# Two-layer transformer/Mamba kernel on eight cores: a second projection pass dropped, reciprocals moved into the score loop, and the Mamba input matmuls run ahead

## What is computed

```python
# layer 0, attention (16 heads of 64), after a layer norm of x
Z = query @ Wz + bz
Z = (Z - mu) * rsqrt(var + 1e-5) * ln_g + ln_b
Q, R, Hv = Z @ Wq + bq, Z @ Wr + br, Z @ Wh + bh        # per head
Qc = concat([Q*cos(Q@Wphi+bphi), Q*sin(Q@Wphi+bphi)])   # Rc alike from R
scores = Qc @ Rc^T
out = (scores / max(sqrt(sum(scores**2)), 1e-12)) @ Hv  # then @ Wo + bo
# layer 0 ffn: shared SwiGLU branch + 8 routed experts
# layer 1, two Mambas (m1 forward, m2 on the reversed sequence)
x, z = split(h @ Win)
x = silu(causal_conv4(x) + bconv)
dbc = x @ Wx;  dt = softplus(dbc[:, :32] @ Wdt + bdt)
h_t = exp(dt*A) * h_(t-1) + dt*B*x;   y = sum_n(h_t * C)   # 16 states
out = ((y + Dp*x) * silu(z)) @ Wout
# layer 1 ffn: int8-quantized product
```

## Time and profile before

| | us |
|---|---|
| median of 2 timed runs | 9415.58 |
| the two runs | 9391.38 and 9439.77 |
| profiled execution, its own time | 9415.49 |
| its span, first to last instruction, slowest core (core 3) | 9414.0 |
| spans of the 8 cores | 9384.4 to 9414.0 |
| busy PE / DVE / ACT / POOL | 4334.1 / 4807.9 / 3167.4 / 172.1 |
| mean granted clock of PE over all cores | 0.624 to 0.629 |

### The profile page before, as it was taken

One profiled execution on the slowest core, in us unless ns is written; L12 is line 12 of the kernel. 1 busy time (PEld: TensorE's weight loads), 2 busy tenths in 40 slices (PEclk: granted clock), 3 DMA queues, 4 the chain that ended last, 5 costly groups with the idle time before them and its releaser, 6 DMA issues.

```text
span 9414.0 us, 57603 instructions; the slowest of 8 cores (9384.4 to 9414.0 us)
## 1 busy us (share of the span) xinstructions
PE 4334.1 (46%) x11136; PEld 1254.8 (13%) x11136; DVE 4807.9 (51%) x8137; ACT 3167.4 (34%) x4433; POOL 172.1 (2%) x221
## 2 busy tenths in 40 slices
PE   3644564456447499994323232323233232323334
PEld 1211111111112142110000000000000000000112
DVE  2434443444444321225476766757575767767345
ACT  3333333333332221003342534434343534344321
POOL 0000000000000000000000000000000000000000
PEclk8766776676768796665555555555555555555556
DMA  1042682100000242110000000000000000000000
GB/s 45 5 38 23 70 84 25 18 0 4 4 0 10 58 128 74 54 45 0 11 7 16 4 17 3 16 7 13 12 9 14 5 18 3 15 6 13 26 11 36
DMA packets 203008, 222.94 MB, mean 24 GB/s; under 512 B 131441, under 2 KB 140049, under 8 KB 200561
## 3 DMA queue, kind: packets, MB, share of 16 engines
q0 software_dynamic: 141104, 76.50, 7.8%
q1 hardware_dynamic: 61570, 142.76, 4.6%
HBM read 278.07 MB, written 65.03 MB: 36 GB/s over the span
## 4 chain that ended last, share of the span: by engine, by line
DVE 39%; PE 31%; issue 14%; ACT 12%; DMA 2%; DVEq 1%; POOL 0%; ACTq 0%; SPq 0%; POOLq 0%
DVE HBF L1731 14%; PE P2U L200 10%; PE PSU L200 6%; DVE DBXP L1727 5%; PE P3U L200 3%; PE PSU L855 3%; PE PSU L866 3%; DVE SCBW L885 2%; DVE XCC L1456 2%; DVEq L35 1%; PE P3U L1783 1%; DVE CARRY L1736 1%; ACT L1655 1%; ACT SCBW L895 1%; PE P3U L1703 1%
## 5 line engine op out<-in xcount | busy, mean ns | idle before, releaser
L1703 PE MATMUL P3U<-DBXP,EYEB 128*128 128x512 bf16 x1024 | 580.1, 566 | 1967.2 <-DVE DBXP L1738 1967.0
L1731 DVE TENSOR_TENSOR_SCAN HBF<-DAP,CARRY,DBXP 128x512 bf16<-128x512 bf16 x1024 | 1314.4, 1284 | 109.3 <-DVE DBXP L1727 3.7
L885 DVE CAST SCBW<-PSU 128x512 bf16<-128x512 f32 x512 | 353.6, 691 | 532.1 <-PE PSU L855 526.8
L1727 DVE TENSOR_TENSOR DBXP<-U_CH,BREP 128x512 bf16<-128x512 bf16 x1024 | 428.8, 419 | 311.4 <-ACT DAP L1655 189.9
L855 PE MATMUL PSU<-QCB,RCB 128*128 128x512 bf16 x1024 | 434.3, 435 | 292.8 <-DVE REP L831 292.8
L866 PE MATMUL PSU<-SCBW,HV 128*64 128x512 bf16 x960 | 415.0, 432 | 196.6 <-DVE SCBW L885 165.0
L895 ACT CAST SCBW<-PSU 128x512 bf16<-128x512 f32 x512 | 300.2, 586 | 526.5 <-PE PSU L855 525.8
L200 PE MATMUL P2U<-YLN,W1E 128*128 128x512 bf16 x512 | 462.1, 1078 | 11.3 <-DMA W1E<-wfsc 11.3
L1667 ACT ACTIVATE DAP<-DT_CH,ACOL 128x512 bf16<-128x512 bf16 x512 | 358.9, 719 | 304.7 <-DVE HBF L1731 299.9
L1703 PEld LDWEIGHTS P3U<-DBXP,EYEB 128*128 128x128 bf16 x1024 | 107.5, 105 | 2448.1 <-issue 2447.9
L1738 DVE TENSOR_TENSOR DBXP<-HBF,CREP 128x512 bf16<-128x512 bf16 x1024 | 424.4, 414 | 1.9 <-issue 1.9
(11 more groups left out here) (324 smaller groups left out, 7176.6 us busy)
## 6 DMA issues: line engine op xcount, KB each, us to landing
wfsc<-L_ffn_w POOLq DMA_DIRECT2D x16, 2048.0 KB, 89.2
SW1H<-wfsc SPq DMA_DIRECT2D x64, 256.0 KB, 2.7
SW3H<-wfsc SPq DMA_DIRECT2D x64, 256.0 KB, 3.0
SW2C<-wfsc SPq DMA_DIRECT2D x32, 512.0 KB, 4.3
W1E<-wfsc SPq DMA_DIRECT2D x8, 2048.0 KB, 12.1
W2E<-wfsc SPq DMA_DIRECT2D x8, 2048.0 KB, 7.7
WINS<-wmsc SPq DMA_DIRECT2D x64, 256.0 KB, 2.6
WINZ<-wmsc SPq DMA_DIRECT2D x64, 256.0 KB, 2.6
```

The source lines that it names most:

```text
L885: b.sV.inc(v.tensor_copy(SCBW[kt % 2][:], PSU[kt % 2][:, :]))
L1703: b.sT.inc(t.matmul(ybank[:, :], EYEB[:], DBXP[ni % 2][:], start=(ni == 0), stop=(ni == 7)))
L1727: b.sV.inc(v.tensor_mul(DBXP[ni % 2][:], U_CH[:, dt * QC:(dt + 1) * QC], BREP[:, ni * QC:(ni + 1) * QC]))
L1731: b.sV.inc(v.tensor_tensor_scan(HBF[ni % 2][:], DAP[ni % 4][:], DBXP[ni % 2][:], CARRY[:, dt * 16 + n: dt * 16 + n + 1], ALU.mult, ALU.add))
```

## The change

It has three parts.

1. **Z stage.** The bf16 copy of Z goes into its place in `ZLN` rather than into `STB`. The statistics matmuls read it there. `_zb_t`, the second pass of 256 matmuls, is gone, and `_zb_v` multiplies the bf16 copy from SBUF by `REP`.
2. **Heads.** Square root, maximum and reciprocal of `RNREP` leave the head's start. Each query chunk does its own 512 columns behind its score casts and ahead of `_av_ev`, in blocks of their own. The mark in `pair_free` for ACT is taken behind the square root.
3. **Mamba.** PE issues the `Win` groups of all eight tiles first, over three `WINS` buffers and three banks (`PSU[0]`, `PSU[1]`, `PSU[3]`), and the eight products with `WXB` behind them (`_s1_t2`). There is one `XCC` and one `ZT` in place of two each, so a convolution waits for the SiLU before it.

```diff
@@ _za_t, _za_v, _zb_v
-                    b.sT.inc(t.matmul(PSU[0][0:1, :], ONECOL[:], STB[2 * (j % 2) + 1][:],
+                    qj, ej = divmod(j, KT)
+                    b.sT.inc(t.matmul(PSU[0][0:1, :], ONECOL[:],
+                                      ZLN[:, ej * T + qj * QC: ej * T + (qj + 1) * QC],
                                       start=(et == 0), stop=(et == KT - 1)))
...
-                    b.sV.inc(v.tensor_copy(STB[2 * (j % 2) + 1][:], ZCH[j % 2][:]))
+                    b.sV.inc(v.tensor_copy(ZLNt(et)[:, q * QC:(q + 1) * QC], ZCH[j % 2][:]))
...
-            b.t(_zb_t)
...
-                    b.sV.inc(v.scalar_tensor_tensor(ZCH[j % 2][:], PSU[2 + j % 2][:, :],
-                                                    BIAS[:, et:et + 1],
-                                                    REP[:, q * QC:(q + 1) * QC],
-                                                    ALU.add, ALU.mult))
+                    b.sV.inc(v.tensor_mul(ZCH[j % 2][:],
+                                          ZLNt(et)[:, q * QC:(q + 1) * QC],
+                                          REP[:, q * QC:(q + 1) * QC]))
@@ heads
-                    b.s(_rne_s)
-                    b.v(_rne_v)
...
                         prev_sc = (b.sV.n, b.sS.n)
+                        def _rnq_s(s, qc=qc):
+                            b.sS.wait(s)
+                            b.sS.inc(s.activation(RNREP[:, qc * QC:(qc + 1) * QC],
+                                                  RNREP[:, qc * QC:(qc + 1) * QC], AF.Sqrt))
+                        b.s(_rnq_s)
+                        rnq_m = b.sS.n
+                        def _rnq_v(v, qc=qc, rnq_m=rnq_m):
+                            b.sS.wait(v, rnq_m)
+                            b.sV.inc(v.tensor_scalar(RNREP[:, qc * QC:(qc + 1) * QC],
+                                                     RNREP[:, qc * QC:(qc + 1) * QC],
+                                                     C_TINY, None, ALU.max))
+                            b.sV.wait(v)
+                            b.sV.inc(v.reciprocal(RNREP[:, qc * QC:(qc + 1) * QC],
+                                                  RNREP[:, qc * QC:(qc + 1) * QC]))
+                        b.v(_rnq_v)
                         if hh == 1 and qc == NQ - 1:
                             pair_free[hp].append((b.sS, b.sS.n))
 
                         def _av_ev(v, qc=qc, hh=hh, hp=hp):
                             b.sT.wait(v)
                             b.sS.wait(v)
+                            b.sV.wait(v)
@@ Mamba stage 1
-                            elif dt >= 2:
-                                b.sT.wait(g, tb6 + 2 * (dt - 2) + 1)
+                            elif dt >= 3:
+                                b.sT.wait(g, tb6 + (dt - 3) + 1)
...
-                            b.sT.inc(mm_group(t, PSU[dt % 2][:, :],
-                                              [(WINS[dt % 2][:, kt * 128:(kt + 1) * 128],
+                            b.sT.inc(mm_group(t, XZB[dt % 3][:, :],
+                                              [(WINS[dt % 3][:, kt * 128:(kt + 1) * 128],
                                                 mv_h(kt, c0, QC)) for kt in range(KT)]))
                             st_tm[dt] = b.sT.n
-                            b.sS.wait(t, st_sm.get(dt, 0))
+
+                    def _s1_t2(t, st_sm=st_sm):
+                        for dt in range(KT):
+                            b.sS.wait(t, st_sm[dt])
                             b.sT.inc(t.matmul(PSU[2][0:64, :],
                                               WXB[:, dt * 64:(dt + 1) * 64],
...
-                            if dt >= 2:
-                                b.sS.wait(v, sb6 + dt - 1)
+                            if dt >= 1:
+                                b.sS.wait(v, sb6 + dt)
...
-                                    if dt >= 2:
-                                        b.sV.wait(s, gate3_m[dt - 2])
+                                    if dt >= 1:
+                                        b.sV.wait(s, gate3_m[dt - 1])
```

More of the change, by code:

```diff
@@ L521, in _za_v @@
                 for j in range(NJ):
+                    q, et = divmod(j, KT)
                     b.sS.wait(v, s_zevac_cnt(j))
-                    b.sV.inc(v.tensor_copy(STB[2 * (j % 2) + 1][:], ZCH[j % 2][:]))
+                    b.sV.inc(v.tensor_copy(ZLNt(et)[:, q * QC:(q + 1) * QC], ZCH[j % 2][:]))
             b.v(_za_v)
             ln_statmath_and_reps(PSU[2], denom=D)
-            z2tb, z2sb, z2vb = b.sT.n, b.sS.n, b.sV.n
-            presnap = b.snap()
-            zb_tm = {}
+            z2sb, z2vb = b.sS.n, b.sV.n
             zb_vm = {j: z2vb + 2 * (j + 1) for j in range(NJ)}
             zb_sm = {j: z2sb + j + 1 for j in range(NJ)}
[L534 to L543, removed]
-            b.t(_zb_t)
             def _zb_v(v):
@@ L814, in build_program @@
                     mm_evac(NQ, rn_mm, rn_ev, [PSU[0], PSU[1]], "s")
[L815 to L821, removed]
-                    b.s(_rne_s)
-                    def _rne_v(v, sb_rn=sb_rn):
-                        for qc in range(NQ):
-                            b.sS.wait(v, sb_rn + qc + 1)
-                            b.sV.inc(v.tensor_scalar(RNREP[:, qc * QC:(qc + 1) * QC],
-                                                     RNREP[:, qc * QC:(qc + 1) * QC],
-                                                     C_TINY, None, ALU.max))
-                            b.sV.wait(v)
-                            b.sV.inc(v.reciprocal(RNREP[:, qc * QC:(qc + 1) * QC],
-                                                  RNREP[:, qc * QC:(qc + 1) * QC]))
-                    b.v(_rne_v)
                     prev_sc = None
@@ L1360, in build_program @@
             p3b = contextlib.ExitStack()
-            WINS = [p3b.enter_context(nc.sbuf_tensor(f"WINS{i}", [128, KT * 128], BF16)) for i in range(2)]
+            WINS = [p3b.enter_context(nc.sbuf_tensor(f"WINS{i}", [128, KT * 128], BF16)) for i in range(3)]
             WINZB = p3b.enter_context(nc.sbuf_tensor("WINZ0", [128, 2 * KT * 128], BF16))
@@ L1364, in build_program @@
             WOUTS = [p3b.enter_context(nc.sbuf_tensor(f"WOUTS{i}", [128, 512], BF16)) for i in range(2)]
-            ZT = [p3b.enter_context(nc.sbuf_tensor(f"ZT{i}", [128, QC], BF16)) for i in range(2)]
+            ZT0 = p3b.enter_context(nc.sbuf_tensor("ZT0", [128, QC], BF16))
+            ZT = [ZT0, ZT0]
             XS_CH = p3b.enter_context(nc.sbuf_tensor("XS_CH", [128, KT * QC], BF16))
@@ L1416, in emit_dir, with _s1_t @@
                     b.y(_s1_g)
-                    def _s1_t(t, ch=ch, dr=dr, st_wm=st_wm, st_sm=st_sm, st_vm=st_vm, c0=c0):
+                    XZB = [PSU[0], PSU[1], PSU[3]]
+                    def _s1_t(t, ch=ch, dr=dr, st_wm=st_wm, st_tm=st_tm, st_vm=st_vm, c0=c0):
                         for dt in range(KT):
                             wait_marks(t, st_wm[dt])
-                            if dt >= 2:
-                                b.sV.wait(t, st_vm[dt - 2])
+                            if dt >= 3:
+                                b.sV.wait(t, st_vm[dt - 3])
                             elif ch > 0 or dr > 0:
@@ L1438, in emit_dir @@
                     b.t(_s1_t)
+                    b.t(_s1_t2)
                     s1_free[0] = b.sT.n
+                    s1_vlast[0] = vb6 + 8 * KT
                     def _s1_v(v, ch=ch, dr=dr, st_tm=st_tm, st_vm=st_vm, c0=c0):
                         for dt in range(KT):
-                            XC = XCC if dt % 2 == 0 else XCC2
+                            XC = XCC
                             b.sT.wait(v, st_tm[dt])
@@ L1492, in _t @@
                                 b.dW.wait(t, wdt_mark)
+                                b.sV.wait(t, s1_vlast[0])
                                 if (6 + j) in dtv1_m:
```

14 lines of the change are left out of this document (7 added, 7 removed).

## The result

The changed kernel takes 9220.8 us (median of 11 runs, 9214.3 to 9279.7) against 9395.4 us for the kernel before run beside it (10 runs, 9389.0 to 9475.7). The ratio is 0.9812, with a 95% interval of 0.9785 to 0.9838: 175 us or 1.9% faster. The forecast was 9234 us and a ratio of 0.981, on the edge of 2%. It started from 9415.5 us for the kernel before, which is 20 us above the median of the ten runs here, so the ratio and the gain are the comparison to make. In some executions the cores of a die run stretches at a granted clock of 0.81 and take longer, so where a small difference matters the two quickest executions of a kernel are given too (9214.3 and 9215.7 us for the changed one).

What follows compares the result with a forecast made beforehand. No engine was taken as the bound everywhere (DVE held 39% of the chain, PE 31%), so each part was priced at its own waits. Z -17, heads +76 and Mamba -240 sum to -181 us, 9415.5 to 9234; range 9180 to 9310.

Steps and rivals of the forecast that it cites:

- The Z stage: Z stage: DVE starts about 3.9 us earlier and a piece takes 1.49 us, -17 us in all, between -23 and -15.
- The heads' start: Start of each head: scores no longer wait for the reciprocal, 17.3 us saved per head, -277 us for 16 heads.
- The gap at a chunk's end: Chunk ends in the heads: square root, maximum and reciprocal make L904 start 5.45 us later, exposed at 57 chunk ends.
- The relief for ACT's table load: Heads: ACT's table load for the next chunk's casts is done during the reciprocal, 48 x -0.3 = -14 us.
- The clock: Heads: later chunks start at PE's lower clock after the gap, 0.75 us for 48 chunks, +44 us with 1 us per pair.
- 1.4 instead of 1.95: Later chunks of a head: a start at the lower clock costs 1.4 us, not the 1.95 of a head's first chunk.
- The rival that the clock stays as it was: Heads: the gaps leave the clock unchanged, so 44 us go, 9190 us; chance 0.18 for both undisturbed-clock forms.
- The rival of a lower clock throughout the chunk: Heads: the lower clock lasts through the chunks, 9386 us; chance 0.10, in part or in full.
- drain: Heads, a rival: each switch of table set adds about 1.38 us, 9300 us with 48 added loads; chance 0.03.
- The heads in all: All terms of the heads together: -277 + 323 - 14 + 44 = +76 us.
- 8 for transposes and projections that start at the lower clock: Heads: transposes and projections that start at the lower clock add 1 us per pair, counted within the +44 us.
- The Mamba stage: Mamba stage 1: PE leaves the turn, a tile takes 5.47 us, 30.0 us saved per chunk, -240 us for 8 chunks.

Runs made afterwards that it cites:

- e3: Only the Z part of the change, made to the kernel before; ratio 0.9976 to the kernel before.
- e4: The changed kernel with 20 extra matmuls on PE in the gap of chunks 2 to 4 of each head; ratio 0.9789 to the kernel before.
- e5: The changed kernel with a chunk's square root in the same ACT block as its casts, behind them; ratio 0.9758 to the kernel before.
- e7: The changed kernel with square root, maximum and the reciprocal in four pieces placed between a chunk's casts; 8863.9 us, ratio 0.9445 to the kernel before.
- e1: Only the heads part of the change, made to the kernel before; ratio 1.0090 to the kernel before.
- e2: Only the Mamba part of the change, made to the kernel before; ratio 0.9742 to the kernel before.

## Why the prediction was right

**The Z stage**, forecast -17, is -19 in the trace: counted from ACT's last copy into `REP` (392.82 before, 391.54 after), the start comes 3.9 us sooner, and 31 pieces take 44.3 us from 392.2 to 436.5 where they took 59.3. e3 gives 0.9976, 23 us (8 to 37). The price of the bf16 by f32 product, for which no row of before existed, was 0.68 for 0.69 taken.

**The heads' start**, forecast 17.3 us a head, is 18.26 - 0.82 = 17.44.

**The gap at a chunk's end**, forecast 5.45 us, is 5.47 by the timeline, 5.46 by e4's quickest chunks (19.93 - 14.47) and 5.51 by the means at clock 1.00 (20.07 - 14.56). e5 shows that the table load is 1.3 of them, and e7 that all of them depend on the place alone.

**The relief for ACT's table load**, -14 us, did not appear. This is the one term that was wrong. A chunk at clock 1.00 in the kernel before, whose L904 starts at 1606.67, and then the one in e4 whose L899 starts at 603.67 show why; the rows are of PE's value matmuls:

```profile
1609.14 0.38 PE L866 MATMUL PSU<-SCBW,HV 128*64 128x512 bf16 x1 [0.34 <-ACT SCBW L895]
...
1609.81 0.38 PE L866 MATMUL PSU<-SCBW,HV 128*64 128x512 bf16 x1
```

```profile
605.73 0.40 PE L843 MATMUL PSU<-SCBW,HV 128*64 128x512 bf16 x1
...
606.81 0.38 PE L843 MATMUL PSU<-SCBW,HV 128*64 128x512 bf16 x1 [0.36 <-DVE SCBW L862]
```

The second value matmul did wait for ACT before (0.34 us) and comes sooner in e4, 2.06 us after the multiplication's start instead of 2.47. But the third comes 3.14 us after it in both, since in e4 PE waits there for DVE's cast. The wait for ACT was not on the path that sets a chunk's length.

**The clock**: the forecast added 0.75 us a chunk, as 14.47 + 1.4 - 15.12. Measured it is 1.22 - 0.56 = 0.66, 4 us less over 48 chunks. Two readings behind the 0.75 were a little off and nearly cancel, which is luck: 14.47 is the quickest chunk at the higher clock and not the mean (14.56), and the start at the lower clock costs 1.2 rather than 1.4. The reason given for 1.4 instead of 1.95, no stall for ACT in the opening, was not tested at the lower clock; at the higher one, as just seen, that stall sets nothing. The rival that the clock stays as it was would need chunk ends 20.6 us apart without help; they are 21.29. The rival of a lower clock throughout the chunk needs over 23. The table load has no drain behind it that a run shows: 597.61 to 598.91 is 1.30 us, and e5 gives back 1.29 us for each load that it takes away.

**The heads in all**, forecast +76, are +83 in the two profiles (first projection matmul to the last L904 or L893: 2518.4 before, 2601.7 after) and +85 in e1. By the terms as measured the sum is -279 + 57 x 5.47 + 7 x 1.7 + 48 x 0.66 = +77. The other 7 us stand where the forecast had 8 for transposes and projections that start at the lower clock; no run takes these apart.

**The Mamba stage**, forecast -240, is -241 from the first SiLU of the first chunk to the last of the last (3721.6 before, 3480.8 after) and -242 in e2.

The three terms measured in the profiles, -19 + 83 - 241, give -177; the measured gain is 175 us and the forecast's was 181. Each part is right by itself. The one wrong term, 14 us, is smaller than the interval of the ratio (25 us to either side), so only the traces could show it.
